# A sixteen-image vision tower: identity products on TensorE ahead of twelve of its waits

## What is computed

```
h = tok(x)
h = h + A(ln(h))      # linear attention, elu feature map
h = h + B(ln(h))      # softmax attention, gated low-rank addition to q, k, v
h = h + C(ln(h))      # attention with a softmax over the head's columns, q and k normalised
h = h + D(ln(h))      # softmax attention and an MLP of 768; second half of the images in three mixed branches
h = h + E(ln(h))      # attention with a second-order polynomial in place of exp
h = h + F(ln(h))      # quantised linear layer
h = h + G(ln(h))      # softmax attention and a layer normalisation
h = h + H(ln(h))      # 8 experts of 192 x 768 x 192, the 2 best of each token
```

## Time and profile before

| | us |
|---|---|
| median of three executions | 641.99 |
| the profiled execution, its own time | 636.27 |
| its span, first to last instruction | 634.5 |
| TensorE busy in it | 557.3 (88%) |
| VectorE, ScalarE, GpSimd busy | 268.1, 215.1, 82.7 |
| mean granted TensorE clock | 0.879 of full speed |

### The profile page before, as it was taken

One profiled execution on the slowest core, in us unless ns is written; L12 is line 12 of the kernel. 1 busy time (PEld: TensorE's weight loads), 2 busy tenths in 40 slices (PEclk: granted clock), 3 DMA queues, 4 the chain that ended last, 5 costly groups with the idle time before them and its releaser, 6 DMA issues.

```text
span 634.5 us, 8990 instructions
## 1 busy us (share of the span) xinstructions
PE 557.3 (88%) x3557; PEld 452.8 (71%) x3557; DVE 268.1 (42%) x684; ACT 215.1 (34%) x441; POOL 82.7 (13%) x85
## 2 busy tenths in 40 slices
PE   4898789796949689899999489399999999999997
PEld 4867658685748577776678368367678877887886
DVE  5476536345763666454447667831201101100101
ACT  0232242223324435435541364552322242243120
POOL 1220100011111010120001310420112211220000
PEclk9998799696968789999999599655559999999999
DMA  8800000000200000000210000002112112101100
GB/s 320 202 2 1 0 2 0 2 1 1 66 1 2 1 1 2 2 1 1 94 82 1 1 2 2 0 14 71 73 51 88 50 38 87 35 2 38 37 0 30
DMA packets 6176, 22.19 MB, mean 35 GB/s; under 512 B 671, under 2 KB 2455, under 8 KB 5946
## 3 DMA queue, kind: packets, MB, share of 16 engines
q1 hardware_dynamic: 5132, 17.51, 8.6%
q10 hardware_dynamic: 1008, 4.18, 2.0%
HBM read 20.78 MB, written 0.91 MB: 34 GB/s over the span
## 4 chain that ended last, share of the span: by engine, by line
PE 73%; DVE 15%; ACT 4%; issue 3%; POOL 2%; DMA 1%; SPq 0%; DVEq 0%; ACTq 0%; POOLq 0%
PE bank L1168 19%; PE bank L1432 12%; PE bank L1381 5%; PE bank L1136 5%; PE bank L1156 5%; PE bank L1114 4%; PE bank L1289 4%; PE bank L1195 3%; PE bank L1333 3%; PE bank L1145 2%; PE bank L1348 2%; ACT xn L513 2%; DVE stats L723 2%; PE bank L1320 1%; PE bank L1393 1%
## 5 line engine op out<-in xcount | busy, mean ns | idle before, releaser
L1432 PE MATMUL bank<-weights,arena_k 128*128 128x192 f32 (+1 forms) x480 | 80.0, 328 | 0.7 <-DVE vblk L1079 0.7
L1079 DVE SCALAR_TENSOR_TENSOR vblk<-bank,disp,vblk 128x192 f32<-128x192 f32 (+1 forms) x40 | 15.2, 413 | 153.6 <-PE bank L1432 153.6
L1432 PEld LDWEIGHTS bank<-weights,arena_k 128*128 128x128 f32 (+1 forms) x480 | 77.2, 183 | 2.1 <-issue 1.0
L1168 PE MATMUL bank<-x_high,w_low 128*128 128x296 f32 x192 | 70.3, 401 | 4.9 <-DVE x_low L759 4.0
L684 ACT ACTIVATE arena_k<-bank,expert_b 128x296 f32<-128x296 f32 x72 | 36.6, 508 | 92.1 <-PE bank L1168 92.1
L415 POOL TENSOR_TENSOR rstd<-rstd_tmp,minus_half 101x4 f32<-101x4 f32 x20 | 20.6, 1028 | 321.3 <-DVE rstd_tmp L733 321.3
L1168 PE MATMUL bank<-x_low,w_high 128*128 128x296 f32 x192 | 59.5, 396 | 0.0
L1168 PEld LDWEIGHTS bank<-x_high,w_low 128*128 128x128 f32 x192 | 41.3, 215 | 25.2 <-issue 25.1
L1156 PE MATMUL bank<-weights,rep 96*111 96x192 f32 (+1 forms) x320 | 56.8, 327 | 0.0
L1156 PEld LDWEIGHTS bank<-weights,rep 96*111 96x111 f32 (+1 forms) x320 | 52.1, 175 | 2.2 <-issue 2.1
L1168 PEld LDWEIGHTS bank<-x_low,w_high 128*128 128x128 f32 x192 | 33.4, 218 | 16.8 <-issue 7.0
(11 more groups left out here) (186 smaller groups left out, 794.4 us busy)
## 6 DMA issues: line engine op xcount, KB each, us to landing
weights<-in_w SPq DMA_DIRECT2D x8, 768.0 KB, 4.3
weights<-in_w ACTq DMA_DIRECT2D x6, 576.0 KB, 3.7
arena_k<-in_patches SPq DMA_DIRECT2D x4, 606.0 KB, 8.3
weights<-in_wpack SPq DMA_DIRECT2D x2, 576.0 KB
weights<-in_wpack SPq DMA_DIRECT2D x1, 1152.0 KB
weights<-in_w SPq DMA_DIRECT2D x2, 576.0 KB, 6.2
weights<-in_wpack SPq DMA_DIRECT2D x1, 1008.0 KB
weights<-in_wpack SPq DMA_DIRECT2D x1, 678.0 KB
```

Source lines behind the costliest of these rows:

```text
L1168: last = mm(ps[:, 0:QT], a, t, start=(y == 0), stop=(y == len(parts) - 1))
L1432: last = mm(PS[4 + c][0:crow[t], D * x:D * x + D], hbuf[b][:, m, 128 * t:128 * t + crow[t]], w2b[:, b, m], start=(m == 0), stop=(m == MT - 1))
```

## The change

Before the wait of twelve phases or steps TensorE now multiplies the 128 x 128 identity by itself, a fixed number of times, into columns 0 to 127 of the bank in which its next job will be. `keep_busy` waits for that bank to be read first, as the job itself would; then come the products, then the wait that stood there before. In eleven places it is `keep_busy`; in the twelfth, ahead of the first `first_hidden`, the products stand in the code and go to bank 0. What the products write is overwritten by the job (`start=True`), and nothing reads it. Nothing else changes.

```
+IDLE_T = {("B", 1): 11, ("D", 1): 8, ("F", 1): 25, ("G", 1): 9, ("H", 0): 10}
+IDLE_R = 19
+IDLE_FC1 = 16
+IDLE_O = {("B", 0): 12, ("C", 0): 12, ("C", 1): 15, ("G", 1): 14}
...
+            def keep_busy(j, n):
+
+                b, k = where[j]
+                if k:
+                    pe.wait_ge(bank_read[b], k)
+                for _ in range(n):
+                    mm(PS[b][:, 0:128], ident, ident, start=True, stop=True)
...
                     wait_evacuated(*[max((j for j in order if where[j][0] == b), key=lambda j: where[j][1]) for b in range(4)])
+                    for _ in range(IDLE_FC1):
+                        mm(PS[0][:, 0:128], ident, ident, start=True, stop=True)
                     for b in range(2):
                         first_hidden(b, X_OCTS[0], b * MT)
...
                 if ph == "T":
+                    if (n, q) in IDLE_T:
+                        keep_busy(("nT", n, q, 0), IDLE_T[n, q])
                     pe.wait_ge(*xn_ready.at((n, q)))
...
                 if ph == "R":
+                    keep_busy(("k", n, q, 0), IDLE_R)
                     wait_evacuated(*[("qk", p) for p in ps8])
...
                 if ph == "O" and n != "A":
+                    if (n, q) in IDLE_O:
+                        keep_busy(("o", n, cs[0]), IDLE_O[n, q])
                     wait_evacuated(*[("v", n, p) for p in ps8])
```

## The result

The change takes 617.66 us (median of four executions, 615.57 to 621.42) against 642.09 us before, measured beside it (four executions). The ratio is 0.963, 95% interval 0.957 to 0.968. So it is faster by 24.4 us, where 37.9 were forecast, and it lies at the upper edge of the range. The profiled execution took 615.57 us, with a span of 613.8 where that of before was 634.5: 20.7 us less. A ratio compares each kernel's faster executions, those within 1.5% of its fastest, so it can differ a little from the ratio of the medians.

A forecast was written before the change was run, and what follows sets the result against it. TensorE bounds the kernel, with 154 us at the lower clock after idle waits. Gains of 20.0 us up to 400 us and 17.9 after make 37.9: 641.99 - 37.9 = 604 us, range 594 to 618.

The forecast's parts named there:

- Up to 117 us: Slow stretch from 72 to 82 us: held clock gives 4.4 us, VectorE's gating of the second half finishing in time.
- The eighth, near 60 us: Low-clock stretch near 60 us, ahead of the seven counted ones: the change does not touch it; no gain counted.
- 117 to 147: Slow stretch from 117 to 127 us: held clock gives 4.1 us, everything being in line on TensorE.
- 147 to 159: Slow stretch from 147 to 157 us: 2.1 us gained, 0.4 from the transposes and 1.7 from the rest.
- only 0.4 comes through: Transposes at 147 us: ScalarE and VectorE build key blocks behind them, scores wait for these, so only 0.4 us is gained.
- 178 to 226: Slow stretches from 178 to 195 and 216 to 226 us: held clock gives 2.6 and 4.2 us.
- 352 to 366: Slow stretch from 352 to 366 us: 3.9 us, less what hides behind quantising on VectorE, leaves 2.6.
- the seven stretches: Low-clock stretches from 72 us on, 146.7 us together, 119.2 busy: said to begin within or just behind the twelve waits.
- 400 to the end: First-layer products, transposes, gate and bias steps from 412.74 us: 20.7 us gained, cut to 17.9 by the compact state's reload.
- rival 2: The clock falls already in the gate; next 30 products stay slow, 14 instead of 17.9 gained, 608 us; chance 0.22.
- a reload wait: Before the bias term: TensorE waits nearly 4 us for the reloaded compact state, cutting the gain from 20.7 to 17.9 us.
- Rival 3: Some places up to 412 us still lose the clock, at most 9.4 in the 60 products: 612 to 622 us; chance 0.12.

The follow-up runs named there:

- the change measured again: The change with no edit, run again in a later session beside the kernel before: 621.0 us, ratio 0.970.
- the filled kernel: The change with products also in waits its profile still showed, some counts raised, two products before each gate block: 613.0 us, ratio 0.957 to the kernel before.
- the last three alone: The change with only the 14, 10 and 16 products around the start of block H kept, 40 of 170: 630.2 us, ratio 0.981 to the kernel before.
- the fastest kernel: The filled kernel with six products instead of two before each gate block and four more short waits filled: 603.8 us, ratio 0.937 to the kernel before.

## Why the prediction was right and wrong

Right in direction and in the mechanism as far as the waits go: the clock was the cost, its return the gain, and no added product overran a wait where the clock was high. No added product had to wait for its bank, and the two waits forecast at 1.8 us came out at 1.71. The step that failed is the one that let the clock fall in waits only, so that filling twelve of them, and nothing else, holds it from 65 to 440 us. It fell in the gate, whose thirty records follow one another behind a wait of 0.88 us, and it fell at two smaller waits (1.97 and 1.76 us). The size of an added product was off by a little: 0.217 us was taken from columns alone; 38 records before the first R last 4.51 us of timeline (141.72 to 146.23), 0.237 us a product. That is below the 0.253 us at which the sum of waits would be used up, and it cost nothing.

The gain was 37.9 us in the forecast and 20.7 between the profiled executions. Starts of the same work in both profiles give the terms:

- Up to 117 us: forecast 4.4 us; block B's O starts at 117.12 instead of 115.85, a loss of 1.3. **5.7 us too much.** The gain of 4.4 us itself came: 4.1 us between block B's second transposes (76.96 for 71.56) and 117 us. In the change measured again only 0.8 of it came, with the fall in block B's gate. But here 4.0 us were lost ahead of the first added product (72.69 for 68.69, where the wait began before), and 1.4 more because the clock stayed low from 56 to 76.5 us, so that the eleven products ran at 0.40 us and overran. "The eighth, near 60 us, the change does not touch" was right; what failed is that I took this stretch to end by itself at 65 us in every execution. It differs between executions of one kernel; why is open.
- 117 to 147: forecast 4.1; 149.50 has become 146.79, 2.7 + 1.3 = 4.0. Right.
- 147 to 159: forecast 2.1, found 0.35. **1.8 too much.** The wait for the key blocks behind the shortened transposes grew to 1.97 us, and the clock fell around it. The prediction had what causes the wait ("only 0.4 comes through") and did not ask what it does to the clock. With eight products in it the scores take 3.22 us: shown by the filled kernel.
- 178 to 226: forecast 2.6 + 4.2, found 2.7 + 4.2. Right.
- 352 to 366: forecast 2.6; 370.48 has become 360.60, no gain over the 10 us before. **2.7 too much.** The products filled the first wait, and the clock then fell among three small ones of 0.73, 0.85 and 1.76 us. The step that failed: "the seven stretches begin within it or just behind it", read as if the twelve waits were all.
- 400 to the end: forecast 17.9, found 20.7 - 9.9 = 10.8. **7.1 too much.** The 60 products gave 9.0 for 9.4, the transposes behind them 0.5 for 0.6. Then the clock fell in the gate, which was rival 2, at a chance of 0.22, priced at 14. The gate gave 2.2 for 3.9; the 30 products, the transposed gates and the bias term gave 0.2 for 6.8; and `fc2` lost 1.1, since the clock came back 3.2 us into it (11.36 us for its first 60). Against this stand the 2.8 us that the forecast had taken off for a reload wait, which did not come up: SyncE's load went out at 429.80 and the bias term began at 436.72, after it.

The terms that missed add up to 5.7 + 1.8 + 2.7 + 7.1 = 17.3, and 37.9 - 17.3 = 20.6. The range was too narrow by one thing more: it took one profile for the kernel. The kernel before spreads from 633 to 645 us over executions, the change from 616 to 624, and the clock's falls lie in other places in each. Rival 3 (the 60 products lose the clock after all) came true in the profile of the change measured again, and not in the first.

SyncE's timeline in the changed kernel, for the reload:

```profile
429.80 0.39 SPq L392 DMA_DIRECT2D vblk<-h_compact  x1
```

The Trainium skill ("TensorE: Matmul & The Clock Gate", Part 1) puts the ramp penalty at less than 1% of a typical kernel span. As the bound on the gain that the prediction made of it, this does not hold here: 4% came back with the change and 6% with the fastest kernel, out of falls in the middle of the run.

Open: why the first stretches differ between executions, how much the eleven products of the first place are worth on the mean, and whether the nine places up to 400 us all pay for themselves. Together those nine are worth the rest of the gain, since the last three alone give 0.981 and all give 0.963 to 0.970; one by one they were not tried.

## To carry to other kernels

Read the granted clock before the busy share: a stretch with a busy TensorE at 0.50 is a stretch at half rate, and look at what stood just before it: here it was a wait, or products of eight columns. Here identity products of 128 columns, put into a wait and counted so that they end before the wait does, held the clock, and sixteen of them ahead of a long slow stretch won it back, even at the price of a little overrun. Look also for stages that lose the clock by themselves, as the gate did, since filling waits does nothing for them, and measure over many executions, because one profile shows one pattern of falls.

## What was not expected of the hardware

- With sixteen identity products begun at the lower level the clock came back after 1.7 us, while 60 first-layer products behind an idle wait ran for 22 us without it, at full busy share.
- 340 transposes held it as well as products did (622.3 and 621.0 us), and in one profile won it back; 170 products of eight columns, busy as long, did not (649.0 us).
- The same program, on the same data, lost the clock in the 60 products in one execution (21.09 us) and kept it in another (13.3 us), with a wait of 1.15 and 1.16 us before them.
